# The attention mask written to the score bank by ScalarE instead of TensorE, with the values product moved behind the projection of v and new instruction orders

## The reference

```python
qkv = x @ Wqkv;  q, k, v = split(qkv, 3)          # 16 heads of 64
q = l2norm(q) * qs;  k = l2norm(k) * ksc
q = q*cos*scale + rotate_half(q)*sin*scale;  k = k*cos*inv + rotate_half(k)*sin*inv
sim = einsum('bhwie,bhwje->bhwij', q, k) * QK_SCALE
sim = where(mask, -max, sim)                       # causal within the 32 tokens
out = softmax(sim) @ v;   x = out @ Wo + x
x = (a * gelu(gate)) @ W2 + b2 + x                 # a, gate = layernorm(x) @ W1 + b1
```

## Time and profile before

| | before |
|---|---|
| median of 3 runs | 2946.76 us (2944.97 to 2947.03) |
| the profiled execution | 2947.82 us, its span 2946.0 us |
| mean granted TensorE clock over the span | 0.982 of full speed |
| TensorE busy | 2734.6 us, 93% |
| VectorE busy | 2611.3 us, 89% |
| ScalarE busy | 2208.1 us, 75% |
| GpSimdE busy | 2141.3 us, 73% |
| the layer loop | from about 403 to 2886 us of the span |

### The profile page before, as it was taken

The page is one execution under the profiler, slowest core; times in us unless marked ns, Lnnn a source line. Parts: engine busy times, 40 slices in busy tenths (PEclk is TensorE's granted clock), DMA queues, the critical chain, the costliest instruction groups (busy, mean ns, idle before and its releaser), DMA issues. The chain is left out here.

```text
span 2946.0 us, 91092 instructions
## 1 busy us (share of the span) xinstructions
PE 2734.6 (93%) x35456; PEld 2117.2 (72%) x35648; DVE 2611.3 (89%) x3407; ACT 2208.1 (75%) x3601; POOL 2141.3 (73%) x1529
## 2 busy tenths in 40 slices
PE   8799978999999999999999999999999999999985
PEld 7688866777777777777777777777777777777763
DVE  6899968999999998989999899999999898989972
ACT  5688857777787878778787877778787877778671
POOL 5777658777787777787777787777877777777750
PEclk9899999999999999999999999999999999999996
DMA  1000013232223222232322232322322322222222
GB/s 53 22 1 1 1 41 76 67 75 67 62 71 74 67 67 69 65 75 65 74 66 66 65 75 68 74 62 67 73 71 60 77 63 66 68 62 62 64 58 62
DMA packets 103839, 178.38 MB, mean 61 GB/s; under 512 B 29222, under 2 KB 52836, under 8 KB 103524
## 3 DMA queue, kind: packets, MB, share of 16 engines
q1 hardware_dynamic: 102500, 174.69, 24.4%
q10 hardware_dynamic: 1152, 1.20, 0.1%
HBM read 22.72 MB, written 2.10 MB: 8 GB/s over the span
## 5 line engine op out<-in xcount | busy, mean ns | idle before, releaser
L1384 POOL TENSOR_TENSOR spare<-spare,qk_t 128x1024 f32<-128x1024 f32 x384 | 912.1, 2397 | 131.5 <-DVE qk_t L1234 121.5
L1218 DVE TENSOR_REDUCE ss<-spare 128x16 f32<-128x1024 f32 x384 | 464.1, 1209 | 73.7 <-ACT spare L990 72.9
L1393 POOL TENSOR_TENSOR spare<-spare,inv 128x1024 f32<-128x1024 f32 x192 | 365.9, 1906 | 209.7 <-ACT inv L1029 209.6
L801 PE MATMUL pa<-w_hi,xs_hi 128*128 128x512 f32 x1152 | 494.0, 429 | 13.5 <-DVE qk_t L1234 6.5
L1225 DVE TENSOR_TENSOR spare<-pa,rot 128x1024 f32<-128x1024 f32 x384 | 465.6, 1212 | 0.4 <-PE px L829 0.3
L801 PE MATMUL pa<-w_hi,xs_lo 128*128 128x512 f32 x1152 | 455.5, 395 | 0.0
L801 PE MATMUL pa<-w_lo,xs_hi 128*128 128x512 f32 x1152 | 453.7, 394 | 0.0
L1234 DVE TENSOR_TENSOR qk_t<-pa,rot 128x1024 f32<-128x1024 f32 x384 | 450.0, 1212 | 0.0
L829 PE MATMUL px<-ident_sb,spare 128*128 128x128 f32 x3072 | 411.0, 277 | 8.2 <-ACT qT L1037 3.9
L829 PEld LDWEIGHTS px<-ident_sb,spare 128*128 128x128 f32 x3072 | 336.8, 140 | 72.3 <-issue 31.9
L1400 POOL TENSOR_TENSOR sm<-sm,inv 128x512 f32<-128x512 f32 x192 | 201.5, 1050 | 214.2 <-DVE sm L1256 213.4
(11 more groups left out here) (158 smaller groups left out, 5910.7 us busy)
## 6 DMA issues: line engine op xcount, KB each, us to landing
kT<-spare SPq DMA_DIRECT2D x384, 256.0 KB, 3.7
pT<-prT SPq DMA_DIRECT2D x768, 64.0 KB, 2.0
w_part<-in_Wqkv SPq DMA_DIRECT2D x40, 192.0 KB, 3.7
wo<-in_Wo SPq DMA_DIRECT2D x6, 512.0 KB, 5.5
c_h<-in_x SPq DMA_DIRECT2D x4, 512.0 KB, 9.3
o_x<-in_x SPq DMA_DIRECT2D x8, 256.0 KB, 4.8
out<-o_out SPq DMA_DIRECT2D x8, 256.0 KB, 4.3
wo<-in_W SPq DMA_DIRECT2D x6, 341.0 KB, 5.2
```

Source lines behind the costliest of these rows:

```text
L801: last = pe.matmul(pa[(u + c) % 2][:, half * 512:half * 512 + 512], x[:, j * P:(j + 1) * P], w[:, at], start=(k == 0), stop=(k == 2))
L1218: dve.reduce_sum(ss[:, c, :], heads(sq), AX.X).then_inc(s[sum_sem], 1)
L1384: pool.tensor_tensor(qk_r[:, c, :], qk_r[:, c, :], qk_t[:, c, :], ALU.add)\
L1393: pool.tensor_tensor(k_r, k_r, over(inv[:, j % 2, 1, :], DH), ALU.mult).then_inc(s["norm_k"], 1)
```

## The change

It does the following.

- TensorE no longer multiplies the mask into the score bank, except once, for the first tile. ScalarE copies `mask_b` into `ps` for every other tile (`write_mask`), after VectorE has read the scores of the tile before; a new semaphore `masked` lets the scores wait for it.
- The values product follows the projection of v instead of preceding it. In the loop on the chip its three waits (`await_probs`) stand in front of the last of the projection's six passes. In the unrolled groups they stand directly in front of the values product.
- The order of work within a tile changes on all four engines.

```diff
+                def await_probs(n, back):
+                    pe.wait_ge(s["pT_loaded"], 16 * TILE_B * (n + 1))
+                    pe.wait_ge(s["v_out"], n + 1)
+                    if not isinstance(n, int) or n + back - 1 < NT:
+                        pe.wait_ge(s["tk_out"], (n + back))
+                    else:
+                        pe.wait_ge(s["oT_lo_ready"], n)
+
-                def project(i, j, c, full, l):
+                def project(i, j, c, full, l, before_last=None):
...
+                            if before_last and half == 1 and k == 2:
+                                before_last()
...
-                        project(i, j, 2, "v_full", l)
+                        project(i, j, 2, "v_full", l, None if isinstance(n, int) else lambda: await_probs(n - back, back))
...
-                def prefill_mask(i, j, back):
-                    n, j, live = tile(i, j, back)
-                    if live:
-                        wait_for(pe, s["sub_done"], n)
-                        pe.matmul(ps[:], ident_b[:], mask_b[:], start=True, stop=False, skip_group_check=True)
-
                 def scores(i, j, back):
                     n, j, live = tile(i, j, back)
                     if live:
+                        if isinstance(n, int) and n == 0:
+                            pe.matmul(ps[:], ident_b[:], mask_b[:], start=True, stop=False, skip_group_check=True)
+                        wait_for(pe, s["masked"], n)
                         pe.wait_ge(s["tq_out"], n + 1)
...
+                def write_mask(i, j, back):
+                    n, j, live = tile(i, j, back)
+                    if live:
+
+                        if not isinstance(n, int) or n > 0:
+                            act.wait_ge(s["sub_done"], n)
+                            act.copy(ps[:], mask_b[:]).then_inc(s["masked"], 1)
```

The new order on TensorE, as a diff of its `body`:

```diff
                     for j in range(GT):
+                        if j == 2:
+                            a_block(i, 2, 0)
                         project_q(i, j, l)
...
                         scores(i, j, 2)
+                        if j == 0:
+                            subtract_mean(i, 2)
                         transpose_q(i, j, 1)
...
-                        if j == 0:
-                            subtract_mean(i, 2)
                         project_k(i, j, l)
...
                         transpose_k(i, j, 1)
+                        if j == 0:
+                            variance(i, 2)
+                        if j == 1:
+                            gate_block(i, 2, 2)
...
-                        if j == 1:
-                            gate_block(i, 2, 2)
-                        if j == 0:
-                            variance(i, 2)
-                        weigh_values(i, j, 3, 1)
-                        if j == 1:
-                            a_block(i, 2, 0)
-                        project_v(i, j, l)
+                        project_v(i, j, l, 3)
+                        weigh_values(i, j, 3)
```

More of the change, by code:

```diff
@@ L653, in stack @@
             cos_q cos_k sin_q sin_k rot_q rot_k norm_k tq_done tq_out tk_done tk_out v_out
-            scores_done top_done sub_done scaled exp_done den_done rden_done probs_done turned pT_loaded pv_done pv_out oT_lo_ready wo_hi_ready wo_lo_ready
+            masked scores_done top_done sub_done scaled exp_done den_done rden_done probs_done turned pT_loaded pv_done pv_out oT_lo_ready wo_hi_ready wo_lo_ready
             wo_done res_attn fs_ready center_done fc_ready fsq_ready var_done fln_done frs_ready fn_mul fn_ready fn_hi_ready fn_lo_ready w1_loaded w1_hi_ready w1_lo_ready
@@ L818, in project_k, with project_v @@
                         project(i, j, 1, "k_full", l)
-                def project_v(i, j, l):
+                def project_v(i, j, l, back):
                     n, j, live = tile(i, j, 0)
@@ L866, in scores, with weigh_values @@
                         last.then_inc(s["scores_done"], 1)
-                def weigh_values(i, j_now, back, mask_back):
+                def weigh_values(i, j_now, back):
                     n, j, live = tile(i, j_now, back)
                     if live:
-                        pe.wait_ge(s["pT_loaded"], 16 * TILE_B * (n + 1))
-                        pe.wait_ge(s["v_out"], n + 1)
-                        if not isinstance(n, int) or n + back - 1 < NT:
-                            pe.wait_ge(s["tk_out"], (n + back))
-                        else:
-                            pe.wait_ge(s["oT_lo_ready"], n)
-                    prefill_mask(i, j_now, mask_back)
-                    if live:
+                        if isinstance(n, int):
+                            await_probs(n, back)
                         for h in range(HEADS):
@@ L1173, in body @@
                         if j == 0:
-                            square_centred(i, 2)
-                            copy_centred(i, 2)
-                        square_k(i, j, 0)
+                            shift_hi(i, 0, 1)
+                        if j == 2:
+                            shift_hi(i, -1, 0)
                         if j == 1:
                             gate_gelu(i, 2, 1)
+                        square_k(i, j, 0)
                         copy_kT(i, j, 1)
@@ L1192, in body @@
                         copy_oT(i, j, 3)
+                        floor_norms(i, j, 0)
+                        copy_v(i, j, 0)
                         if j == 0:
                             scale_shift(i, 2)
+                        log_norms(i, j, 0)
+                        if j == 2:
+                            round_part(l, g)
+                        if j == 0:
                             round_normed(i, 2)
-                        floor_norms(i, j, 0)
-                        if j == 1:
-                            round_part(l, g)
                 act.preload_act_table_set(EXP_LN)
@@ L1319, in body @@
                     for j in range(GT):
-                        if j == 1:
-                            rest_of_normed(i, 2)
-                        if j == 2:
-                            gated(i, 2, 1)
+                        if j == 3:
+                            add_ffn(i, 2)
+                        maximum(i, j, 2)
                         turn_probs(i, j, 3)
-                        maximum(i, j, 2)
                         sum_squares(i, j, 0, 0, "sq_q", "sum_q")
@@ L1452, in body @@
                         norm_keys(i, j, 0)
+                        if j == 0:
+                            shift_lo(i, 0, 1)
                         if j == 2:
-                            shift_lo(i, -1, 0)
                             rest_of_part(l, g)
```

37 lines of the change are left out of this document (18 added, 19 removed).

## The result

The changed kernel takes 2909.99 us (median of 4 runs, 2903.21 to 2911.15), against 2946.68 for the kernel before on the same chip. The ratio is 0.9873 [0.9861, 0.9885]: 1.3% faster, 37 us. The prediction said 2894 us, 53 us less; its range (2825 to 2950) holds the result. The sign and, in j=1, the place of the new waits and their owners came out as written. The gain forecast is 1.4 times the measured one.

The account below looks back on a forecast made before the run. TensorE bound: 48.6 us of work plus 2.5 of stalls a group, VectorE close at 46.9. Group 51.1 to 50.0, times 48 groups: 53 us; 2947.8 - 53 - 1.1 = 2894 us, range 2825 to 2950.

Parts of the forecast that it names:

- The mask: On TensorE: each mask product costs 0.22 us; removing four saves 0.88 us a group, 42 us over 48 groups.
- rival C: Mask's time isn't given back but turns into longer waits; only 10 us gained, 2937 us; chance 8%.
- The 0.10: Change to small products before the values product: 0.10 us stays in the 0.33 us gap, loads waiting behind a full-height pass.
- The copy on ScalarE: 191 mask copies into the score bank, 0.5 us each, 2 us a group, hidden except in j=1 behind the second table load.
- The values product behind v: Keys' copy (1.05 us) then lies beside five passes (1.15 us), so TensorE's 1.0 us stall in j=0 goes.
- The walk through one group: New orders followed through four loop tiles: 10.3 + 12.5 + 13.1 + 14.1 = 50.0 us, against 51.1 before.
- The two chains that were to meet in j=1: Keys' DMAs let scores start at 13.1, VectorE's subtraction ends at 14.0; together 1.2 us of TensorE stall.
- the hand-over: Between values product and next transposition: ScalarE's copy and VectorE's subtraction need 2.4 of 2.5 us, so no cost.
- The stalls that remain: One of 2.5 us of TensorE stalls a group removed, nearly the same put back by keys' DMAs and VectorE's chain.
- The gelu's 0.4: In j=1 gate products and gelu alternate as before, costing TensorE 0.4 us of stall.
- From the group to the kernel: The walked group's gain of 1.1 us applied to all 48 groups: 53 us.
- still ends 0.8 us ahead of the keys' transposition: GpSimdE starts each tile's rotation some 1.6 us later, yet finishes 0.8 us before TensorE transposes the keys.

Follow-up runs that it names:

- e2: Changed kernel with the mask product back on TensorE, between the projection of v and the values product, no ScalarE copy: 2931.75 us, ratio 0.9954.
- e5: Kernel before, old orders and place, with no mask at all (attention not causal), an 8-column product carrying the waits: 2932.55 us, ratio 0.9952.
- e1: Kernel before, old orders and place, but the mask copied by ScalarE, an 8-column product carrying the waits: 2949.35 us, ratio 1.0017.
- e6: Changed kernel with no mask at all, neither copy nor product (attention not causal): 2908.01 us, ratio 0.9874.
- e3: Changed kernel with the values product ahead of the projection of v again, an 8-column product carrying its waits: 2944.26 us, ratio 0.9997.
- e7: Kernel before, old orders, with the mask copied by ScalarE and the values product moved behind the projection of v: 3034.04 us, ratio 1.0299.
- x4: Changed kernel with two groups in each loop turn, three turns a layer instead of six: 2979.47 us, ratio 1.0115.
- x6: Changed kernel with VectorE's subtraction fn_lo behind the maximum of j=1 instead of ahead of it: 2908.27 us, ratio 0.9875.

## Why the prediction was right, and where its size was off

**The mask (right as work, not as a gain of its own).** 0.22 us a product stands: e2's gaps give 0.23. As TensorE's work the 0.88 us a group hold too: 47.7 us of work and 2.4 of stalls make the 50.1 that the loop takes. But the mask's move alone gives back 0.54 in the new orders (e2), and in the old ones 0.26 without the copy (e5) and nothing with it (e1). The rest turns into waits for the keys' DMA, VectorE and ScalarE. That was rival C, given 8% and held to be the opposite of the forecast; it is true of about half the saving in three of the four tiles. The 0.33 us in front of the values product stayed, as forecast. The prediction took the 0.10 in it as weight loads that wait behind a full-height pass. That can't hold of every load: in the kernel before a projection's load starts at 1417.97 and lasts 0.19 us, beside the full-height pass that started at 1417.96, and the passes still follow each other at 0.23.

**The copy on ScalarE (right).** 0.59 us long, 0.53 from start to start, hidden (e6). That it is hidden is owed to the new orders: in the old ones it costs 0.36 us a group (e1 against e5).

**The values product behind v (right).** The wait for the keys' copy ahead of it is gone, and e3 prices the place at 0.94 us. That this is near the 1.0 of the prediction is in part luck: it is what is left of two stalls in e3 (0.65 and 0.98 us of idle time), less the 0.8 us before the scores and the 0.33 at the loop's turn that the new place brings, and a stall before the transposition that is longer in e3. The price holds only with the new orders: without them the same move costs 53.12 - 51.23 = 1.9 us (e7).

**The walk through one group (right to 0.2 us a tile).** Tiles of 10.3, 12.5, 13.1 and 14.1 us were predicted. In the changed kernel the tiles of this group start at 0, 10.4, 22.7 (in j=2 the a product stands ahead of q's projection), 35.8 and 50.1, so 10.4, 12.3, 13.1 and 14.3. The two chains that were to meet in j=1 do meet. In j=3, where no stall was expected, TensorE waits 0.17 us for VectorE's subtraction: the hand-over, walked with 0.1 us to spare, misses by that, since VectorE is at the denominators when ScalarE's copy ends. Zero, the start of q's projection in j=0, lies at 1403.03 for this group: the scores of j=1 start at 1415.85 - 1403.03 = 12.8 (walked 13.1), the subtraction ends at 13.9 (walked 14.0), and the gate product starts at 15.4 (walked 15.3). VectorE's part:

```profile
1414.93 0.68 DVE L1274 TENSOR_REDUCE den<-pr 128x16 f32<-128x512 f32 x1
1415.64 0.25 DVE L1277 RECIPROCAL rden<-den 128x16 f32<-128x16 f32 x1
1415.81 1.16 DVE L1305 TENSOR_TENSOR oT_lo<-px,oT_hi 128x1024 fp32r<-128x1024 f32 x1
1417.29 1.13 DVE L1299 TENSOR_TENSOR fn_lo<-fx,fn_hi 128x512 fp32r<-128x512 f32 x1 [0.31 <-ACT fn_hi L1145]
```

**The stalls that remain (sum off by 0.1, contents by more).** 2.3 us a group were predicted (50.0 - 47.7), 2.4 are there. In j=1 (each gap between starts less that of undisturbed work): 0.85 before the scores, 0.24 before the transposition, 0.50 before the gate. Two terms were missing. fn_lo was walked at 0.7 us and took 1.13 (median of the 48), beside GpSimdE's product:

```profile
1416.80 1.07 POOL L1433 TENSOR_TENSOR pr<-pr,rden 128x512 f32<-128x512 f32 x1
```

That is 0.45 us on the way to the gate. The other is the turn of the loop: it costs TensorE 0.3 us a group behind the values product, where in the old order it was hidden (0.23 us from pass to pass, at the turn as elsewhere). 30 turns x 0.3 = 9 us. The gelu's 0.4 fell to almost nothing, so that the sum hardly moved; that the walk came out within 0.2 us is in part luck. The Trainium skill says this of the first term (SBUF — State Buffer, Who interferes with whom): a VectorE instruction with two SBUF inputs contends with a GpSimdE instruction that reads SBUF. The traces agree, in both directions: 0.68 to 1.13 and 1.44 us on VectorE, or 1.05 to 1.37 on GpSimdE. The walk took VectorE's duration from the kernel before, where the two met for 0.13 us only, and didn't ask what would run beside it in the new place.

**From the group to the kernel (mis-sized).** This is the step that failed: the sum took 1.1 us for all 48 groups. The loop groups gave 27.5 us in 30 periods, 0.92 each. The 17 others gave 10.4, 0.6 each, and the 12 unrolled groups among them only 4.4 together; the first two groups of the first layer lost 3.3 us. This is the largest part of the 15 us that are missing: 17 x 1.1 = 19 were expected there, 8 more than came. The loop gave 5.5 less than 30 x 1.1, and the 48th group is the last 1.1. The prediction spoke of the unrolled groups once, about where the waits stand, and took the rest of them from a group it had not walked.

What the trace shows there: in the unrolled groups the changed kernel's TensorE waits 17.7 us before the scores for the keys' DMA (5.1 before the change), and 9.8 us, in 11 cases, before a transposition for the keys that GpSimdE normalises; in the 36 loop groups the second wait doesn't occur. So the walk's statement on GpSimdE, that it "still ends 0.8 us ahead of the keys' transposition", holds in the loop only. The longest case, in the first layer's second group, with TensorE first and GpSimdE below, and then the wait in the whole span:

```profile
453.48 1.59 PE L840 MATMUL px<-ident_sb,spare 128*128 128x128 f32 x8 [2.33 <-POOL spare L1404]
...
451.52 1.91 POOL L1404 TENSOR_TENSOR spare<-spare,inv 128x1024 f32<-128x1024 f32 x1
...
PE px L840 <- POOL spare L1404: 11.4, 12, 2.3
```

GpSimdE had been busy with hardly a gap from 443.29 to 453.43, with none of it on weights: the scores, the rest of the input (xs_lo), the rotations, the probabilities, the keys. Behind this stand TensorE's granted clock was at half for 6.8 us, and the group took 53.2 us. In x4 and x6 the stand is the same 2.33 us but the clock was at half for 3.4 us, and the group took 51.2 and 51.6. So some 2 us of what the first layer loses there go with the clock, and differ from profile to profile. A later wait of the same kind in that group (1.23 us at 478.64) does have weights behind it: GpSimdE's work on wo_lo, 2.40 us from 467.64, delays its rotations.

**Left open.** How the 6.6 us that the 12 unrolled groups give less than 12 x 0.92 divide between the keys' DMA, GpSimdE and the clock. Also open is the end of the kernel: what follows the last start of a group took 141 to 149 us in the profiles of these kernels, the longer the more of it ran at half the clock (49 to 51 us of it in the shortest two, 65 to 73 in those over 146); so a single profile's span can't settle 5 us.

## What to carry to other kernels

Price a product removed from the fullest engine tile by tile: it counts in full only where that engine sets the pace, and turns into waiting where a chain through the others ends last. Parts of a change can be worth nothing or worse without the others (the mask alone 0, mask and place without the orders +3%, mask and orders without the place 0) and pay together, so they can't be judged one at a time. When an instruction is moved, look at what the neighbour engines do at its new time, not only at its own duration; and walk the unrolled groups as well as the loop's.

## What the runs showed of the hardware that I had not expected

- The turn of a loop costs TensorE 0.3 us when small products (64 columns) stand ahead of it, and nothing visible when 512-column passes do: 1.43 against 1.10 us in the changed kernel, 0.23 from pass to pass in the kernel before.
- A loop body of two groups (some 190 KB of TensorE's instructions) made TensorE stand for 5.3 us at each of 12 turns, against 1.43, and moved 5.08 MB of instructions in place of 1.90. The body of one group (some 93 KB) ran without reloading.
- A VectorE subtraction of 128x512 with both inputs in SBUF takes 0.63 to 0.69 us alone. Where GpSimdE's instruction on SBUF is already running, the subtraction stands still and ends 0.55 us after that instruction: 1.13, 1.44 and up to 2.41 us. When it starts first, GpSimdE's product pays instead (1.37 for 1.05).
